# Order of the query tile blocks within a pair of attention heads: 6+1, 7+0, 4+3, 5+2 in place of 7+0, 6+1, 5+2, 4+3

## The chip, the cores and the metric

The kernel runs on one core of a Trainium2 chip. The metric is the device time of one execution in microseconds. The kernel before takes 1441.79 us (median of 3 runs, 1440.93 to 1442.77); lower is better.

## The reference

The input is x, four sequences of 1024 tokens with 256 channels, float32. It is normalised over the channels (xn), and the result is

```python
x = x + attention(xn) + einsum('bsi,oi->bso', xn, binarised(W_ffn)) + b_ffn
```

The attention has 16 heads with compressed keys, values and queries:

```python
kv_c = x @ W_kvd + b_kvd                       # 64 channels
keys = concat(heads(kv_c @ W_ku + b_ku), rope(heads(kv_c @ W_kr + b_kr)))    # 128 + 64 per head
q_c  = x @ W_qd + b_qd                         # 192 channels
q    = concat(heads(q_c @ W_qu + b_qu), rope(heads(q_c @ W_qr + b_qr)))
scores = einsum('bhqd,bhkd->bhqk', q, keys) / sqrt(192), masked above the diagonal
ctx = einsum('bhqk,bhkd->bhqd', softmax(scores), heads(kv_c @ W_vu + b_vu))
return ctx @ W_o + b_o
```

The mask is causal: query tile qt (128 rows) sees only key tiles 0 to qt.

## The kernel before

All matmuls keep float32 quality by splitting operands in a high and a low part (fp32r) and adding products. The 16 heads are handled in 8 pairs per sequence, so there are 4 x 8 = 32 pair steps. `LONG_SHORT` (line 48) cuts the 8 query tiles of a pair into 4 blocks, each of a long and a short tile: (7, 0), (6, 1), (5, 2), (4, 3). Each block has 9 key tiles per head in sum. Blocks are numbered g = 0 to 127; the position of a block in its pair is n = g % 4 (positions 0 to 3), and every table by n (which tiles, which output is stored) reads `LONG_SHORT[n]`.

What one block does:

- TensorE writes scores into two PSUM slots used in turn (`ring`), in four items: x = 0 is head 0 of the long tile, x = 1 head 0 of the short tile, x = 2 and 3 the same for head 1. An item is a mask matmul on its diagonal tile (L1457) and three matmuls (high x high, low x high, high x low) for each chunk of up to 512 key columns (L1474 to L1476). The mask of an item is issued within an earlier group of transposes and waits until the item two before it has left its slot.
- VectorE takes the scores out of PSUM and finds each row's minimum (L1035, function `minimum`; the signs are turned). ScalarE applies the exponent in place and sums the rows (L755, `exponent`).
- TensorE transposes the probabilities in five groups per block (L1499, `turn_group`). A group is up to two key tiles of both heads, four transposes; a long tile with 7 or 5 key tiles, or a short one with 1 or 3, ends with a single group of two transposes. The first group of a tile waits for the exponents of both heads. ScalarE copies the group out as the high part (L764), VectorE subtracts for the low part (L1045).
- TensorE weighs the compressed values with them (L1517, L1518, `weigh_group`) into u_ps; ScalarE and VectorE take that out in two parts (L769, L778, L1051); TensorE multiplies with the value and output weights (L1537, L1538, `output`); VectorE adds the result, scaled by one over the row sum, to `acc` (L1082).

The work is pipelined over blocks. Each engine has a function `sequence(g)` with one list per position n, written out by hand. While block g has its scores made, groups of block g - 1 are transposed and weighed and outputs of g - 2 are made. ScalarE's, VectorE's and TensorE's queues run in order. The lists of position 0 and 1 on TensorE also hold the projections for the next pair: keys for the rotary part (`k_rope`) at the start of position 0, q_x late in position 0, q_y early in position 1 (L1444). ScalarE takes them out (L670); SyncE swaps halves of them with four DMAs (L375); GpSimd does the rotary arithmetic (L347) and the low parts (L357); ScalarE makes high parts (L733, L737). In pairs 5 to 8 of a sequence the lists hold the next sequence's work: statistics and normalisation, its transposes (pair 6), down projections and ffn matmuls (pair 7), natural-order projections (pair 8).

Key columns per chunk: tile 4 has its two chunks 384 and 256 wide, the others 512 and the rest. For both blocks of positions 0 and 1 the long tile has four groups and the short one one; for positions 2 and 3 it is three and two, which the lists assume.

Of the kernel before, what the change touches and what calls it, by code (L numbers as in the profile page):

```python
# [38 lines left out]
NT = SEQ // P  # L39
# [5 lines left out]

LONG_SHORT = tuple((NT - 1 - n, n) for n in range(NT // 2))
BLOCKS = len(LONG_SHORT)
SCORE_ITEMS = 4  # L50
DRAIN = 3
# [3 lines left out]
KEY_COLUMN = {qt: P if qt == 4 else 0 for qt in range(NT)}  # L55
assert all((long + 2) // 2 + (short + 2) // 2 == GROUPS for long, short in LONG_SHORT)

# [74 lines left out]
def build(nc, x, W_kvd, b_kvd, W_ku, b_ku, W_vu, b_vu, W_kr, b_kr, W_qd, b_qd, W_qu, b_qu, W_qr, b_qr,  # L132
# [21 lines left out]
    with ExitStack() as ctx:  # L154
# [143 lines left out]
        def groups_of(g):  # L298

            return [(w, qt, kt, min(2, qt + 1 - kt)) for w, qt in enumerate(LONG_SHORT[g % BLOCKS])  # L300
                    for kt in range(0, qt + 1, 2)]

        def probs_of(g, w, h):

            long, short = LONG_SHORT[g % BLOCKS]
            return probs[g % 2][h][:, (long + 1) * P * w:][:, 0:((long, short)[w] + 1) * P]
# [54 lines left out]
        def _(sp):  # L361
# [65 lines left out]
            def store(b, n):  # L427

                sp.wait_ge(acc_ready, (((b + 1) * PAIRS - 1) * BLOCKS + n + 1) * 2)
                for qt in LONG_SHORT[n]:  # L430
                    sp.dma_start(out[b, qt * P:(qt + 1) * P, :], acc[:, qt, :]).then_inc(stored[n], 16)
# [551 lines left out]
        def _(dve):  # L983
# [40 lines left out]
            def minimum(g, x):  # L1024
# [4 lines left out]
                b, pair, n = g // (PAIRS * BLOCKS), g // BLOCKS % PAIRS, g % BLOCKS  # L1029
                qt, entry = LONG_SHORT[n][w], ("score", g, x)  # L1030
                keys, r = (qt + 1) * P, (g * SCORE_ITEMS + x) % 8
# [765 lines left out]
```

## Time and profile before

| | before |
|---|---|
| median of the runs | 1441.79 us |
| the profiled execution: its time / its span | 1437.33 / 1435.5 us |
| TensorE matmul busy | 1395.9 us (97%) |
| TensorE weight load busy | 1264.1 us (88%) |
| ScalarE busy | 1203.7 us (84%) |
| VectorE busy | 1152.2 us (80%) |
| GpSimd busy | 996.0 us (69%) |
| mean granted TensorE clock | 0.997 |

Rows of the profile name a line of the kernel, an engine, an operation and what it writes from what it reads. PE is TensorE's matmuls, PEld its weight loads, which run beside them; ACT is ScalarE, DVE VectorE, POOL GpSimd. Times in a timeline count from the span's start. A matmul's time there includes its way through the array, so the start-to-start distance of matmuls, not their own time, is what each costs in the stream.

### The profile page before, as it was taken

How to read it: one execution, taken by the hardware profiler on the slowest of the kernel's cores; microseconds unless marked ns; L12 is line 12 of the kernel's file. 1: busy time of each engine (PE TensorE's matmuls, PEld its weight loads, DVE VectorE, ACT ScalarE, POOL GpSimd, SP SyncE). 2: the span in 40 equal slices, each digit the busy share in tenths (PEclk: the TensorE clock that was granted, in tenths of full speed). 3: DMA queues.
4: the chain of work that ended last, by engine and by line, in shares of the span. 5: the costliest groups of instructions: out<-in, count | busy, mean ns of one | idle time of the engine just before them, and what ended most of it. 6: DMA issues, size and time to landing. Idle time of an engine off the chain costs nothing.

```text
span 1435.5 us, 27603 instructions
## 1 busy us (share of the span) xinstructions
PE 1395.9 (97%) x9786; PEld 1264.1 (88%) x9786; DVE 1152.2 (80%) x2708; ACT 1203.7 (84%) x2603; POOL 996.0 (69%) x573
## 2 busy tenths in 40 slices
PE   6989999999999999999999999999999999999997
PEld 4779999998898999988898999999889999999987
DVE  4858888876778888887687889887677888888887
ACT  4668888996888988898688888999778988888886
POOL 6886687777566767768765777777765777666750
PEclk9999999999999999999999999999999999999999
DMA  9752212212333222211333222221233322221100
GB/s 273 213 131 57 74 42 63 63 52 60 83 98 78 78 63 64 63 48 31 77 92 97 67 68 62 64 63 49 63 74 89 87 58 64 63 63 49 41 20 30
DMA packets 46958, 106.82 MB, mean 74 GB/s; under 512 B 9334, under 2 KB 17831, under 8 KB 46823
## 3 DMA queue, kind: packets, MB, share of 16 engines
q1 hardware_dynamic: 43360, 94.01, 25.7%
q0 software_dynamic: 3296, 11.01, 2.7%
q8 instruction: 80, 1.31, 0.4%
q14 instruction: 56, 0.45, 0.1%
q10 hardware_dynamic: 166, 0.03, 0.0%
HBM read 48.92 MB, written 9.96 MB: 41 GB/s over the span
## 4 chain that ended last, share of the span: by engine, by line
PE 77%; ACT 8%; POOL 6%; DVE 4%; DMA 3%; issue 1%; SPq 1%; POOLq 0%; DVEq 0%; ACTq 0%
PE turn L1499 15%; PE ring L1444 10%; PE u_ps L1517 8%; PE ring L1476 8%; PE ring L1475 8%; PE u_ps L1518 8%; PE ring L1474 8%; PE o_ps L1537 4%; PE o_ps L1538 4%; ACT probs L755 3%; PE ring L1457 2%; POOL k_rope L347 2%; PE ring L1389 1%; PE ring L1383 1%; ACT probs_hi L764 1%
## 5 line engine op out<-in xcount | busy, mean ns | idle before, releaser
L1035 DVE TENSOR_SCALAR_CACHE_REDUCE probs<-ring,c_t 128x1024 f32<-128x1024 f32 (+7 forms) x512 | 414.1, 810 | 99.6 <-PE ring L1476 95.4
L1045 DVE TENSOR_TENSOR probs_lo<-turn,probs_hi 128x512 fp32r<-128x512 f32 (+1 forms) x640 | 401.0, 630 | 69.3 <-ACT probs_hi L764 64.4
L764 ACT ACTIVATE probs_hi<-turn 128x512 fp32r<-128x512 f32 (+1 forms) x640 | 349.9, 550 | 110.0 <-PE turn L1499 103.4
L755 ACT ACTIVATE probs<-probs,row_min 128x1024 f32<-128x1024 f32 (+7 forms) x512 | 394.1, 771 | 11.8 <-DVE probs L1035 9.4
L1499 PE MATMUL turn<-ident,probs 128*128 128x128 f32 x2304 | 388.0, 275 | 6.3 <-ACT probs L755 4.0
L1517 PE MATMUL u_ps<-probs_hi,kv_nat 128*128 128x256 f32 x1152 | 313.5, 301 | 0.0
L1499 PEld LDWEIGHTS turn<-ident,probs 128*128 128x128 f32 x2304 | 282.9, 140 | 32.3 <-ACT probs L755 9.9
L1518 PE MATMUL u_ps<-probs_lo,kv_nat 128*128 128x256 f32 x1152 | 288.8, 280 | 0.0
L1474 PE MATMUL ring<-k_hi,q_hi 128*128 128x512 f32 (+3 forms) x768 | 275.8, 359 | 0.0
L1476 PE MATMUL ring<-k_hi,q_lo 128*128 128x512 f32 (+3 forms) x768 | 263.2, 343 | 0.0
L1475 PE MATMUL ring<-k_lo,q_hi 128*128 128x512 f32 (+3 forms) x768 | 262.6, 342 | 0.0
L1082 DVE SCALAR_TENSOR_TENSOR acc<-o_ps,row_inv,acc 128x256 f32<-128x256 f32 x480 | 230.1, 479 | 34.8 <-PE o_ps L1538 30.4
L1517 PEld LDWEIGHTS u_ps<-probs_hi,kv_nat 128*128 128x128 f32 x1152 | 219.1, 190 | 0.7 <-DVE kv_nat L1022 0.3
L1518 PEld LDWEIGHTS u_ps<-probs_lo,kv_nat 128*128 128x128 f32 x1152 | 218.4, 190 | 0.0
L357 POOL TENSOR_TENSOR k_lo<-k_rope,k_hi 64x1024 fp32r<-64x1024 f32 x62 | 148.2, 2390 | 50.1 <-ACT k_hi L733 47.7
L347 POOL TENSOR_TENSOR k_rope<-k_rope,cos 128x1024 f32<-128x1024 f32 x31 | 74.5, 2403 | 143.4 <-DMA swapped<-k_rope 143.1
L347 POOL TENSOR_TENSOR q_x<-q_x,cos 64x1024 f32<-64x1024 f32 x31 | 74.2, 2394 | 131.0 <-DMA swapped<-q_x 131.0
L1476 PEld LDWEIGHTS ring<-k_hi,q_lo 128*128 128x128 f32 x768 | 144.8, 189 | 13.9
L1474 PEld LDWEIGHTS ring<-k_hi,q_hi 128*128 128x128 f32 x768 | 146.6, 191 | 7.4
L347 POOL TENSOR_TENSOR swapped<-swapped,sin 128x1024 f32<-128x1024 f32 x62 | 148.7, 2398 | 4.9
L1475 PEld LDWEIGHTS ring<-k_lo,q_hi 128*128 128x128 f32 x768 | 145.4, 189 | 7.5
L1537 PE MATMUL o_ps<-wv,u_hi 128*128 128x256 f32 x512 | 143.6, 302 | 4.2 <-DVE acc L1082 2.3
(218 smaller groups left out, 2573.7 us busy)
## 6 DMA issues: line engine op xcount, KB each, us to landing
swapped<-k_rope SPq DMA_DIRECT2D x128, 128.0 KB, 2.3
wv<-wv_scratch SPq DMA_DIRECT2D x62, 256.0 KB, 4.1
wp<-wp_scratch SPq DMA_DIRECT2D x62, 192.0 KB, 3.5
wp<-wp_scratch SPq DMA_DIRECT2D x31, 256.0 KB, 3.2
swapped<-q_y SPq DMA_DIRECT2D x62, 128.0 KB, 2.3
swapped<-q_x SPq DMA_DIRECT2D x62, 128.0 KB, 2.4
k_hi<-qb_kv_hi SPq DMA_DIRECT2D x16, 256.0 KB, 3.7
k_lo<-qb_kv_lo SPq DMA_DIRECT2D x16, 256.0 KB, 4.8
```

Of the source, the lines that this page charges most:

```text
L347: engine.tensor_tensor(to, a, b, op).then_inc(rope_step, 1)
L755: act.activation(p, p, ACT.Exp, scale=-1.0, bias=row_min[:, r:r + 1], accum_out=row_sum[:, g % 4, w, h:h + 1]).then_inc(exp_ready, 1)
L764: act.activation(probs_hi[:, r % 4, 0:width], turn[r % 2][:, 0:width], ACT.Identity).then_inc(turned_hi, 1)
L1035: dve.tensor_scalar(probs_of(g, w, h), ring[slot_of(entry)][:, KEY_COLUMN[qt]:KEY_COLUMN[qt] + keys], c_t[b % 2][:, qt, ds(pair * 2 + h, 1 ...
L1045: dve.tensor_tensor(probs_lo[:, r % 4, 0:width], turn[r % 2][:, 0:width], probs_hi[:, r % 4, 0:width].bitcast(F32), ALU.subtract).then_inc ...
L1082: dve.scalar_tensor_tensor(out=acc[:, qt, :], in0=o_ps[:, h, :], scalar=inv, in1=start[:, qt, :], op0=ALU.mult, op1=ALU.add).then_inc((acc ...
L1474: pe.matmul(to, qh, kh[:, keys], start=not masked, stop=False, skip_group_check=masked)
L1475: pe.matmul(to, qh, kl[:, keys], start=False, stop=False, skip_group_check=masked)
L1476: mm = pe.matmul(to, ql, kh[:, keys], start=False, stop=True, skip_group_check=masked)
L1499: mm = pe.transpose(turn[r % 2][:, (2 * t + h) * P:(2 * t + h + 1) * P], probs_of(g, w, h)[:, kt * P:(kt + 1) * P], ident[:, :])
L1517: pe.matmul(u_ps[:, 0:2 * P], kv_nat[:, kt, :], probs_hi[:, r % 4, cols], start=(kt == 0), stop=False)
L1518: mm = pe.matmul(u_ps[:, 0:2 * P], kv_nat[:, kt, :], probs_lo[:, r % 4, cols], start=False, stop=(kt == qt))
```

## The change

One line changes: the order in which the pairs of tiles are listed. The same four blocks exist as before; the position of each within a pair of heads is another, and all lists by position now meet other tile sizes. The stores to DRAM by position follow.

```diff
-LONG_SHORT = tuple((NT - 1 - n, n) for n in range(NT // 2))
+LONG_SHORT = tuple((NT - 1 - n, n) for n in (1, 0, 3, 2))
```

Position 0 holds 6+1 (before: 7+0), position 1 holds 7+0 (6+1), position 2 holds 4+3 (5+2), position 3 holds 5+2 (4+3).

## Rows read from the trace of the kernel before

**Rows 1.** The page's first part: engine, busy us (share), number of instructions.
```profile
PE 1395.9 (97%) x9786; PEld 1264.1 (88%) x9786; DVE 1152.2 (80%) x2708; ACT 1203.7 (84%) x2603; POOL 996.0 (69%) x573
```

**Rows 2.** Waits, whole run: who waited for whom, us in total, times, longest.
```profile
POOL k_rope L347 <- DMA swapped<-k_rope: 143.1, 28, 8.7
...
PE ring L1457 <- ACT q_y L670: 4.0, 2, 3.1
PE turn L1499 <- ACT probs L755: 4.0, 7, 0.9
```

**Rows 3.** TensorE, groups by form: shapes and count, busy us, mean ns, idle before.
```profile
L1476 PE MATMUL ring<-k_hi,q_lo 128*128 128x512 f32 x320 | 126.5, 395 | 0.0
...
L1476 PE MATMUL ring<-k_hi,q_lo 128*128 128x384 f32 x192 | 65.1, 339 | 0.0
```

**Rows 4.** Timeline of TensorE, pair 18, position 2: start us, us, instructions.
```profile
830.35 0.27 PE L1499 MATMUL turn<-ident,probs 128*128 128x128 f32 x1
...
831.63 0.60 PE L1499 MATMUL turn<-ident,probs 128*128 128x128 f32 x4
831.98 0.37 PE L1517 MATMUL u_ps<-probs_hi,kv_nat 128*128 128x256 f32 x1
...
832.87 0.28 PE L1518 MATMUL u_ps<-probs_lo,kv_nat 128*128 128x256 f32 x1
...
833.10 0.28 PE L1518 MATMUL u_ps<-probs_lo,kv_nat 128*128 128x256 f32 x1
833.36 0.55 PE L1499 MATMUL turn<-ident,probs 128*128 128x128 f32 x3
```

**Rows 5.** ScalarE, groups by form: the exponent of 768 and of 640 elements.
```profile
L755 ACT ACTIVATE probs<-probs,row_min 128x768 f32<-128x768 f32 x64 | 59.3, 926 | 0.0
L755 ACT ACTIVATE probs<-probs,row_min 128x640 f32<-128x640 f32 x64 | 52.8, 825 | 0.2 <-DVE probs L1035 0.2
```

**Rows 6.** Timeline of ScalarE, pair 18, positions 2 and 3.
```profile
830.83 0.38 ACT L764 ACTIVATE probs_hi<-turn 128x256 fp32r<-128x256 f32 x1 [0.29 <-PE turn L1499]
...
832.29 0.92 ACT L755 ACTIVATE probs<-probs,row_min 128x768 f32<-128x768 f32 x1
833.12 0.18 ACT L755 ACTIVATION_READ_ACCUMULATOR probs<-probs,row_min 128x1 f32 x1
833.21 0.57 ACT L764 ACTIVATE probs_hi<-turn 128x512 fp32r<-128x512 f32 x1
...
842.33 0.19 ACT L755 ACTIVATION_READ_ACCUMULATOR probs<-probs,row_min 128x1 f32 x1
```

**Rows 7.** VectorE, groups by form: the minimum over 768 and 640 elements.
```profile
L1035 DVE TENSOR_SCALAR_CACHE_REDUCE probs<-ring,c_t 128x768 f32<-128x768 f32 x64 | 64.7, 1011 | 0.7 <-PE ring L1476 0.7
L1035 DVE TENSOR_SCALAR_CACHE_REDUCE probs<-ring,c_t 128x640 f32<-128x640 f32 x64 | 55.4, 865 | 2.2 <-PE ring L1476 2.2
```

**Rows 8.** Timeline of TensorE, pair 18 position 3, pair 19 position 0.
```profile
837.74 0.22 PE L1457 MATMUL ring<-mask_bf,ident_bf 128*128 128x128 bf16 x1
...
843.02 0.49 PE L1499 MATMUL turn<-ident,probs 128*128 128x128 f32 x3
```

**Rows 9.** Timeline of VectorE, pair 18, position 3.
```profile
837.06 0.08 DVE L1035 DVE_READ_ACCUMULATOR probs<-ring,c_t 128x1 f32 x1
```

**Rows 10.** Timeline, position 1 of pair 11 (first row) and of pair 19.
```profile
518.47 0.10 PEld L1457 LDWEIGHTS ring<-mask_bf,ident_bf 128*128 128x128 bf16 x1 [0.33 <-ACT q_y L670]
...
858.98 1.12 ACT L670 ACTIVATE q_y<-ring,bias_p 128x1024 f32<-128x1024 f32 x1 [0.55 <-PE ring L1444]
...
860.91 0.22 PE L1457 MATMUL ring<-mask_bf,ident_bf 128*128 128x128 bf16 x1
```

**Rows 11.** Timeline of TensorE, pair 16, position 3.
```profile
756.11 0.23 PE L1457 MATMUL ring<-mask_bf,ident_bf 128*128 128x128 bf16 x1 [0.94 <-DVE probs L1035]
```

**Rows 12.** Timeline of TensorE, pair 1, position 1.
```profile
94.89 0.29 PE L1457 MATMUL ring<-mask_bf,ident_bf 128*128 128x128 bf16 x1 [3.12 <-ACT q_y L670]
```

**Rows 13.** Busy us by engine (instructions), granted clock, DMA share, GB/s of a window.
```profile
94.00:99.00 5.00, 4.11 (x20) 3.81 (x20) 3.02 (x7) 3.97 (x9) 1.12 (x1) 0.66 0.56 115
```

## The prediction

> **What bounds the kernel now.** I read the page's busy times first, then who waited for whom, then the timelines of one ordinary pair in the middle of the run, pair 18 of 32, position by position. TensorE is busy 1395.9 of 1435.5 us [rows 1]. Its waits are few: the two kinds that this change touches, for the q_y eviction and for the exponent, sum to 4.0 us each [rows 2]. So TensorE's own issue stream is the bound, and only two things can move the time: the sum of that stream, and the small stalls in it. ScalarE matters although it is busy only 84% of the span. In the third and fourth block of a pair its instructions stand back to back, so what it finishes late there TensorE must wait for.
>
> **What is moved, and what it sums to.** The four blocks of a pair hold tiles 7+0, 6+1, 5+2, 4+3. The code that orders each engine's work belongs to the position (n = 0 to 3), not to the tiles. Now position 0 gets 6+1, 1 gets 7+0, 2 gets 4+3, 3 gets 5+2. Every instruction of a pair is still issued once, so the stream's sum stays. Inside a position these sizes change:
> - Scores: 128 key columns more or less on a tile change three matmuls by about 56 ns each [rows 3], 0.17 us; between 128 and 256 columns it is some 0.07 us.
> - The group of two score tiles that is not full. It holds one key tile: two transposes and two u_ps matmuls in place of four and four. It is the last group (index 4) of 7+0 and 5+2, index 3 of 6+1, index 2 of 4+3. A double group takes four transposes, 0.35 us from start to start (831.63 to 831.98 in rows 4), a single about 0.22 us less; a pair of u_ps matmuls is 0.23 us (832.87 to 833.10).
> - ScalarE: 128 more elements of exponent are 0.10 us [rows 5], a double group's eviction 0.57 against 0.38 us [rows 6]. VectorE: 128 more elements of the minimum are 0.14 us [rows 7].
>
> Summed on TensorE: position 0: +0.24, position 1: -0.24, position 2: +0.46, position 3: -0.46 us. As each stays attached to its place, the pair's sum is 0. I cost no DMA: SyncE issues the same transfers in the same order.
>
> **Position 2, the stall of every ordinary pair.** Now the first turn of the block's own probabilities (833.36, three transposes) waits for ScalarE's second long exponent, whose accumulator read ends at 833.12 + 0.18 = 833.30 [rows 4, 6]. TensorE was ready at 833.10 + 0.12 = 833.22, and the first transpose is followed by another 0.06 us of gap: 0.20 us per pair, in 23 of 32 pairs (not in pairs 6 to 8 of the first three batches). It is tempting to book this as gained, because the long tile there shrinks from 6 to 5 key tiles. But the chain starts elsewhere: from turn group 3 (830.35) through its eviction (830.83), the copy and the short tile's exponent, then the long one (832.29), all back to back. With the change group 3 is double (transposes +0.22, eviction +0.20), the short exponent is 512 in place of 384 (+0.10), the long one -0.10: chain +0.42. TensorE from the same point: group 3 +0.22, short scores +0.17, group 4 single -0.22, last weighing double +0.24: +0.41. Stall 0.2 us as before. Bounds: 0 (all of it gone) to 0.4.
>
> **Position 3 into position 0.** From that exponent on ScalarE runs without a gap to the end of position 3's second long exponent, 842.33 + 0.19 = 842.52; the turn that needs it starts at 843.02 [rows 6, 8]: 0.50 us of slack. With the change, after the position 2 stall: group 4's eviction -0.20, third exponent +0.10, position 3: long +0.10, group 2 -0.20, short -0.10, group 4 +0.20, long +0.10: sum 0.0. TensorE between the two points: position 3 is 0.46 shorter, the rest the same. So 0.46 of 0.50 us goes, and 0.04 is left, where a released transpose shows a lag of 0.06 (833.30 to 833.36). That is a stall of 0 to 0.15 us; I take 0.10, the lag and the 0.06 behind it that the like stall in position 2 shows, less 0.03 for a wait on the q_x eviction at the end of position 0 that goes. 0.07 x 23: +1.6 us. In the same block the mask matmul of the third score item sits at 837.74, 0.60 us after the minimum it needs (837.06 + 0.08) [rows 8, 9]. It comes 0.46 sooner (group 2 single -0.22, short scores -0.17, weighing of group 4 of the block two before -0.24, long scores +0.17), the minimum ends 0.05 later: 0.1 us is left, lag of 0.06 included, still no stall.
>
> **The q_y eviction in position 1.** ScalarE's backlog arrives at position 0 about 0.40 us later relative to TensorE (0.46, less 0.10 for the shorter last exponent, plus 0.05 for the minimum), so the k_rope eviction, its swap DMAs, the rope on GpSimd, k_hi, and then q_y all move by 0.40. On GpSimd this goes into its next wait for a swap, of which there are 28 with 143.1 us, 5.1 each [rows 2]. Position 1 starts 0.24 later. Usual q_y ends at 858.98 + 1.12 = 860.10, and the mask needs it at 860.91 [rows 10]: slack 0.81. With the change the mask comes 0.34 sooner in its position (single group 3 -0.22, short scores -0.07, weighing of group 4 of the block two before -0.23, long scores +0.17), and q_y 0.18 later, as its projection starts behind the longer scores: slack 0.28. That is enough in a usual pair. In 6 of the 31 pairs a swap DMA lands about 1.4 us late and the slack is gone already; one such stands at 518.47, where the load of the mask matmul sat idle for 0.33 us until q_y [rows 10]. There k_hi and q_y run back to back, 0.1 us later than now in the position, and the mask comes 0.35 sooner: 0.45 us longer each, +2.2 us for the five in ordinary places. The three pairs in which ScalarE also normalises the next batch there (pair 6 of a batch) have 0.35 of slack and lose 0.15 each: +0.5.
>
> **Once per batch and once per run.** Pair 8 of the first three batches: the mask in position 3 waits for the short minimum [rows 11]; the mask is reached 0.44 sooner, the minimum ends 0.06 sooner, and position 0 behind it then has no stall (-0.07): +0.3 each, +0.9 us. First pair: TensorE waits 3.12 us for q_y at 94.89 [rows 12], a chain from the residual on GpSimd that the order doesn't touch; 0.3 us of TensorE work passes from before this wait to behind it: +0.3. The drain of the last block runs with no scores to cover waits: its group 2 is double (transposes, eviction and subtraction, some 0.6 us by rows 4 and 6), its last group single (-0.6), its long exponent and minimum longer (+0.24), its short ones shorter: -0.5 to +1.2, I take +0.5, as the longer items come first and TensorE runs out of other work behind them.
>
> Sum: 1.6 + 2.2 + 0.5 + 0.9 + 0.3 + 0.5 = +6.0 us. The profiled execution took 1437.33 us (span 1435.5 and 1.8 around it), 4.5 below the median of the runs, 1441.79; 1437.3 + 6.0 = 1443.3 for a like execution. Carried to the median: 1441.8 + 6.0 = 1447.8.
>
> **A rule beside the trace.** In the first pair TensorE, idle for 3.12 us before 94.89, then ran at a mean granted clock of 0.66 between 94 and 99 us, one stretch at 1.2 GHz, the rest at 2.4; at most (1 - 0.66) x 5 = 1.7 us lost [rows 12, 13]. The Trainium skill, "TensorE: Matmul & The Clock Gate", Part 1, says that the throttled clock is the default and that activity releases it; the trace agrees. By that rule a wait that grows is a risk beyond its length: this one grows by 0.3 us, and a second low stretch would be worth up to 1.7 us by the rows. I leave it out of the sum.
>
> **Rivals.**
> - A: faster. The 0.20 us stall of position 2 vanishes and nothing takes its place: -0.2 x 23 = -4.6, and -0.03 x 31 = -0.9, against the +0.3 of the first pair: 1441.8 - 5.2 = 1436.6 us. It is decided by ScalarE's chain from turn group 3: it must end 0.15 us sooner against TensorE than I sum. For it: the long tile is smaller there. Against it: rows 6 have no gap in which the double eviction would fit.
> - B: no change. The small slacks hold (0.04 in position 0, 0.28 in position 1), the late swaps fall where there is room, and only the fixed terms stay, 0.9 + 0.3 + 0.5 = 1.7: 1443.5. For it: the sum of the stream is equal.
> - C: clearly slower. The thin slacks of position 3 and 0 both break: 0.15 us more at each in 23 pairs, 6.9 on top of the 6.0: 1454.7. VectorE would be the new bound in position 3: its first minimum has 768 elements there, it stands behind a subtraction, and both the mask and ScalarE's first exponent wait for it.
>
> **How the numbers follow.** Forecast case 0.50 (its own range 1445 to 1451), A 0.10, B 0.25, C 0.15. What this kernel's measurement tells from no change is 0.2%, 2.9 us. Slower: the forecast, C and a little of B, 0.64; same 0.26; faster 0.10. The range takes in B and part of C: 1441 to 1453.
>
> **What would show it.** In the changed trace of an ordinary pair: the first turn of position 2 still right behind an exponent; TensorE's wait for ScalarE in the first turn of position 0 near 0.1 us; the position 1 mask closer than 0.4 us to q_y's end, with waits for q_y grown from 4.0 us to 6 or more; positions lasting 13.8, 10.4, 9.0 and 6.7 us in place of 13.5, 10.6, 8.5 and 7.2. It is wrong if no exponent ends just before position 2's turn, or if the pair's period falls below 39.8 us.

## The result, and the profile after

The changed kernel takes 1451.15 us (median of 4 runs, 1450.46 to 1452.09), the kernel before 1442.28 us beside it (4 runs, 1440.93 to 1445.14): ratio 1.0069, 95% interval [1.0048, 1.0091]. It is slower, by 8.9 us between these medians, where +6.0 was forecast. (The ratio is given as recorded; the quotient of the two medians is 1.0062.) Run once more later, on the same chip as other experiments, it gave 1.0079 [1.0061, 1.0097]. The profiled execution took 1450.46 us (span 1448.7), 13.2 us of span more than the profiled execution of before.

The page's first part after, as [rows 1]:

```profile
PE 1404.0 (97%) x9786; PEld 1265.2 (87%) x9786; DVE 1148.8 (79%) x2708; ACT 1204.4 (83%) x2603; POOL 995.3 (69%) x573
```

The instruction counts are those of before. TensorE's busy time nevertheless grew by 8.1 us. A row's own time (0.27 us for a transpose) is longer than its distance to the next one (0.11 us), so a wait shorter than the difference leaves no idle time in the profile, and matmuls at the lower clock take longer and count as busy too. Busy time is no measure of work here.

The waits of the whole run after (who waited for whom, us in total, times, longest), as [rows 2]:

```profile
POOL k_rope L347 <- DMA swapped<-k_rope: 150.5, 28, 10.1
...
PE ring L1457 <- ACT q_y L670: 8.1, 5, 4.7
PE ring L1457 <- DVE probs L1035: 6.6, 7, 1.4
PE turn L1499 <- ACT probs L755: 4.8, 8, 1.0
```

The wait for q_y doubled (4.0 to 8.1 us), and the forecast wanted 6 or more. That is weaker than it looks: 4.7 of the 8.1 us are the first pair's (3.1 before), and in a second execution of the same kernel, below, this line reads 1.7 us. The wait for VectorE's minimum (5.7 us before) is the line that the forecast did not put first.

**An ordinary pair.** Lengths of the positions, from the first matmul of a position's list on TensorE to that of the next, median over pairs 1 to 4 of batches 2 to 4 (the last row is the sum of the four):

| position | before | forecast | after |
|---|---|---|---|
| 0 | 13.53 | 13.8 | 13.85 |
| 1 | 10.59 | 10.4 | 10.34 |
| 2 | 8.53 | 9.0 | 9.08 |
| 3 | 7.17 | 6.7 | 6.74 |
| pair | 39.82 | | 40.01 |

Pair 18 after, position 2: ScalarE's second long exponent, and the turn and masks on TensorE behind it (as [rows 4, 6]):

```profile
839.99 0.82 ACT L755 ACTIVATE probs<-probs,row_min 128x640 f32<-128x640 f32 x1
840.71 0.18 ACT L755 ACTIVATION_READ_ACCUMULATOR probs<-probs,row_min 128x1 f32 x1
...
840.95 0.55 PE L1499 MATMUL turn<-ident,probs 128*128 128x128 f32 x3
```

The read ends at 840.89 and the turn starts 0.06 later: the stall of position 2 is still there. Position 3 of the same pair, VectorE, ScalarE and TensorE (as [rows 8, 9]):

```profile
843.24 0.68 DVE L1045 TENSOR_TENSOR probs_lo<-turn,probs_hi 128x512 fp32r<-128x512 f32 x1
843.84 1.01 DVE L1035 TENSOR_SCALAR_CACHE_REDUCE probs<-ring,c_t 128x768 f32<-128x768 f32 x1
844.77 0.09 DVE L1035 DVE_READ_ACCUMULATOR probs<-ring,c_t 128x1 f32 x1
...
844.32 0.59 ACT L764 ACTIVATE probs_hi<-turn 128x512 fp32r<-128x512 f32 x1
844.89 0.94 ACT L755 ACTIVATE probs<-probs,row_min 128x768 f32<-128x768 f32 x1
...
844.78 0.27 PE L1499 MATMUL turn<-ident,probs 128*128 128x128 f32 x1
844.91 0.23 PE L1457 MATMUL ring<-mask_bf,ident_bf 128*128 128x128 bf16 x1
```

The minimum ends at 844.86. The mask follows at 844.91 and the exponent at 844.89: where before [rows 8, 9] the mask came 0.60 us after its minimum, it now comes 0.05 after it. The exponent ends the row at the start of position 0 of pair 19, where the first turn had 0.50 us of slack in [rows 6, 8]:

```profile
850.00 0.19 ACT L755 ACTIVATION_READ_ACCUMULATOR probs<-probs,row_min 128x1 f32 x1
...
850.25 0.98 PE L1499 MATMUL turn<-ident,probs 128*128 128x128 f32 x7
```

It has none: 850.19 to 850.25. And q_y in position 1 of pair 19, as [rows 10]:

```profile
866.64 1.12 ACT L670 ACTIVATE q_y<-ring,bias_p 128x1024 f32<-128x1024 f32 x1 [0.59 <-PE ring L1444]
...
868.06 0.22 PE L1457 MATMUL ring<-mask_bf,ident_bf 128*128 128x128 bf16 x1
```

868.06 less 867.76 is 0.30 us of slack; 0.28 was forecast (0.81 before).

**Where a swap lands late**, pair 14, position 1, first ScalarE, then the load and the mask on TensorE:

```profile
639.48 2.14 ACT L733 ACTIVATE k_hi<-k_rope 64x1024 fp32r<-64x1024 f32 x2 [1.41 <-POOL k_rope L347]
642.65 1.09 ACT L670 ACTIVATE q_y<-ring,bias_p 128x1024 f32<-128x1024 f32 x1
...
643.79 0.10 PEld L1457 LDWEIGHTS ring<-mask_bf,ident_bf 128*128 128x128 bf16 x1 [1.70 <-ACT q_y L670]
643.80 0.23 PE L1457 MATMUL ring<-mask_bf,ident_bf 128*128 128x128 bf16 x1 [1.51 <-ACT q_y L670]
```

**Pair 8 of a batch, position 3**, TensorE, as [rows 11] (the second row is the same place one batch later):

```profile
759.75 0.27 PE L1499 MATMUL turn<-ident,probs 128*128 128x128 f32 x1
761.36 0.23 PE L1457 MATMUL ring<-mask_bf,ident_bf 128*128 128x128 bf16 x1 [1.34 <-DVE probs L1035]
...
1106.22 0.23 PE L1457 MATMUL ring<-mask_bf,ident_bf 128*128 128x128 bf16 x1 [1.36 <-DVE probs L1035]
```

The windows behind them (busy us by engine and instructions, then the granted clock, DMA share, GB/s):

```profile
760.00:765.00 5.00, 3.66 (x27) 3.46 (x27) 2.44 (x8) 3.27 (x8) 4.79 (x3) 0.89 0.03 8
1105.00:1110.00 5.00, 3.78 (x26) 3.60 (x27) 2.32 (x9) 3.13 (x7) 4.79 (x3) 0.86 0.02 3
```

The clock fell from 2.4 to 1.2 GHz at 763.9 and at 1108.6 us, each time for 3.4 us. Before, it fell nowhere between the first pair and the end. Position 3 lasts 11.56 and 11.58 us with the fall and 10.00 in the first batch, where none came: 1.5 us each.

**The 13.2 us of span by part**, pair by pair against the profiled execution of before, with the forecast's terms:

| part | forecast | profiled execution |
|---|---|---|
| ordinary pairs (21), their own period | +1.6 | 0.2 each, +4.2 |
| swaps landing late in them, and one stall of before in pair 9 (0.7) that is not there | +2.2 | +0.3 |
| pair 6 of a batch (3) | +0.5 | +0.6 |
| pair 7 of a batch (3) | 0 | +1.7 |
| pair 8 of a batch (3) | +0.9 | +1.4, and +3.0 by the clock |
| first pair | +0.3 | +1.0 |
| last pair and drain | +0.5 | +0.9 |

The parts sum to 13.1; rounding and 0.03 us ahead of the first pair make up the rest.

### The profile page after: what moved, and what is told of

Same layout as the page of the kernel before. It is cut to its first block, busy times and chain, and to the rows that moved or that the text cites. A ratio compares the mean times of both kernels' runs of the same rounds, so it can differ in the third digit from the quotient of the medians.

```text
span 1448.7 us, 27603 instructions
## 1 busy us (share of the span) xinstructions
PE 1404.0 (97%) x9786; PEld 1265.2 (87%) x9786; DVE 1148.8 (79%) x2708; ACT 1204.4 (83%) x2603; POOL 995.3 (69%) x573
## 3 DMA queue, kind: packets, MB, share of 16 engines
q8 instruction: 80, 1.31, 0.4%
## 4 chain that ended last, share of the span: by engine, by line
PE 73%; ACT 10%; POOL 6%; DVE 4%; DMA 4%; issue 1%; SPq 1%; POOLq 0%; DVEq 0%; ACTq 0%
PE turn L1499 15%; PE ring L1444 9%; PE u_ps L1517 7%; PE ring L1476 7%; PE ring L1475 7%; PE u_ps L1518 7%; PE ring L1474 7%; PE o_ps L1537 3%; PE o_ps L1538 3%; ACT probs L755 3%; POOL k_rope L347 2%; PE ring L1457 2%; DMA swapped<-k_rope 2%; ACT probs_hi L764 2%; PE ring L1389 1%; PE ring L1383 1%
## 5 line engine op out<-in xcount | busy, mean ns | idle before, releaser
L1035 DVE TENSOR_SCALAR_CACHE_REDUCE probs<-ring,c_t 128x896 f32<-128x896 f32 (+7 forms) x512 | 413.5, 809 | 115.5 <-PE ring L1476 112.9
L755 ACT ACTIVATE probs<-probs,row_min 128x896 f32<-128x896 f32 (+7 forms) x512 | 394.7, 772 | 12.8 <-DVE probs L1035 9.1
```

What stands on the lines that cost most here:

```text
L755: act.activation(p, p, ACT.Exp, scale=-1.0, bias=row_min[:, r:r + 1], accum_out=row_sum[:, g % 4, w, h:h + 1]).then_inc(exp_ready, 1)
L1035: dve.tensor_scalar(probs_of(g, w, h), ring[slot_of(entry)][:, KEY_COLUMN[qt]:KEY_COLUMN[qt] + keys], c_t[b % 2][:, qt, ds(pair * 2 + h, 1 ...
```

## The experiments

All were timed against the kernel before on the same chip. The experiments ran in three groups; the median of the kernel before was 1438.55, 1438.48 and 1439.01 us in them (single executions 1434.99 to 1444.86).

**The two halves of the change, each alone.** Positions 0 and 1 exchanged:

```diff
-LONG_SHORT = tuple((NT - 1 - n, n) for n in range(NT // 2))
+LONG_SHORT = tuple((NT - 1 - n, n) for n in (1, 0, 2, 3))
```

> Only positions 0 and 1 are exchanged (6+1, 7+0, 5+2, 4+3). Theory 1 (sizes at fixed places decide, through ScalarE's back-to-back chain): position 2 now transposes the groups of 7+0, so turn group 3 is double there (+0.42 us on ScalarE's chain) while TensorE gains only 0.23 us before the turn that waits for the exponent: the stall of position 2 grows from 0.20 to about 0.4 us in ordinary pairs, position lengths about 13.3, 10.6, 8.95, 6.95 us, the pair 40.0 us; q_y's slack about 0.5 us, so late swaps cost 0.2 us more each. Sum +5 to +7 us on the kernel before (+0.4%). Theory 2 (each exchange costs about half of what the full change costs): +4.5 us, with waits spread over positions 0 and 3 too. Theory 3 (the cost of the full change is mostly the clock falling behind the wait in position 3 of pair 8): the wait there is 1.3 us or less here; if the clock falls, 1.5 us each time, otherwise next to nothing over theory 1.

1450.9 us, 1.0085 [1.0071, 1.0100]. Positions 13.42, 10.61, 9.20 and 6.94 us, the pair 40.17. The whole loss of the change is in this half, and its ordinary pair is longer than with both halves. Theory 1 has the mechanism: the stall of position 2 (the wait at the turn and the gap behind it) grew from 0.20 to 0.38 us. It was too low in the sum, +12 us against +5 to +7; one fall of the clock (1.5 us) and 0.6 us in each pair 7 are part of the difference.

Positions 2 and 3 exchanged, `for n in (0, 1, 3, 2)`:

> Only positions 2 and 3 are exchanged (7+0, 6+1, 4+3, 5+2). Theory 1: in position 2 group 3 stays single, ScalarE's two exponents before the waiting turn sum to the same, and TensorE has 0.17 us more scores in front of it: the stall falls from 0.20 to under 0.05 us; position 0's first turn keeps about 0.2 us of slack, the q_y slack is about 0.6 us. Ordinary pair 39.65 us, sum -3 to -5 us on the kernel before (-0.3%), unless the wait in position 3 of pair 8 (1.3 us expected) lets the clock fall, 1.5 us each. Theory 2 (half the cost each): +4.5 us. Theory 3 (clock): no fall, then within 0.1% of before or faster.

1437.13 us, 0.9988 [0.9976, 1.0000]: at most a small gain, 1.4 us between the medians where -3 to -5 were expected. Positions 13.99, 10.34, 8.38 and 6.93 us, the pair 39.64. The stall of position 2 is down to 0.04 us, as theory 1 wanted. Per ordinary pair +0.35 and -0.18 make +0.17, of the +0.2 of both together: the halves add, nearly.

**The mask in position 3 of pair 8.** The natural-order projection, whose slot is free earlier, stands behind that wait. In the changed kernel it is issued first:

```diff
-                    turn_group(g - 1, 2, (g, 2))
                     if pair == 7:
                         begin("natural", b + 1, 1)
+                    turn_group(g - 1, 2, (g, 2))
```

> The changed kernel (6+1, 7+0, 4+3, 5+2) with one step moved on TensorE: in position 3 of pair 8 the natural-order projections (1.8 us of matmuls) are issued before the group of transposes whose mask waits for the short minimum, not behind it. The wait of 1.5 us there should be covered whole, three times, and with it the falls to 1.2 GHz behind it (1.5 us each, two in the profiled execution). Theory 3 and my account: -4.5 us for the waits and -3 us for the clock, together -7 to -8 us on the changed kernel, so within 0.2% of before. If the clock falls for another reason than this wait, only -4.5 us and the falls stay in the trace.

1442.48 us, 1.0027 [1.0014, 1.0040]. The position lasts 8.66 to 8.68 us in all three batches (10.00, 11.56, 11.58), and the clock falls nowhere in mid-run. By the ratios (1.0069 and 1.0079 down to 1.0027) 6 to 7.5 us were to be had at one place that comes three times.

The same edit in the kernel before:

> The kernel before with the same step moved. There the wait is 1.1 us three times and the clock does not fall: -3.3 us (-0.23%) if TensorE's stream is the bound behind it, with no change in the number of falls. If the wait only moves on to the next turn of position 0, nothing is gained.

1435.74 us, 0.9982 [0.9969, 0.9995]. The position is 1.11 shorter three times, and position 0 behind it 0.36 longer. So some 2.6 of the 6 to 7.5 us (0.7 to 4.5 by the interval) were there to be had before the change already; the other 3.5 to 5 us are what the changed order lost here: 0.4 us more wait three times, and the clock.

**What makes the clock fall.** The changed kernel, with 14 transposes of the identity (result unused) ahead of that mask (the call passes `fill=14` in pair 8 of the first three batches and nothing elsewhere):

```diff
                         if (t, h) == (tiles - 1, 1):
+                            for _ in range(fill):
+                                pe.transpose(turn[r % 2][:, 2 * P:3 * P], ident[:, :], ident[:, :])
```

> The changed kernel with 14 transposes of the identity, whose result nobody reads, issued ahead of the waiting mask matmul in position 3 of pair 8 (three times in the run). They take some 1.2 us and stand in a wait of 1.5 us. Theory (behind this wait TensorE's granted clock falls to 1.2 GHz for 3.4 us in some executions, 1.5 us each, because TensorE stood still; the wait is set by VectorE's minimum and not by TensorE): position 3 of pair 8 lasts 10.0 us in all three batches, no clock fall there, the run 0 to 4.5 us below the changed kernel, 3 likeliest; ratio to the kernel before about 1.005. Rival (the fall has another cause, such as the amount of work before it): falls stay in one or two of three, position 3 at 11.5 there, ratio as the changed kernel or 0.1% above.

TensorE in position 3 of pair 16, and the window over it:

```profile
762.14 0.27 PE L1502 MATMUL turn<-ident,probs 128*128 128x128 f32 x1
762.25 1.69 PE L1499 MATMUL turn<-ident 128*128 128x128 f32 x14
763.77 0.22 PE L1458 MATMUL ring<-mask_bf,ident_bf 128*128 128x128 bf16 x1
```
```profile
760.00:766.00 6.00, 6.00 (x53) 5.83 (x52) 4.76 (x14) 4.63 (x9) 4.25 (x3) 1.00 0.13 44
```

From the transpose ahead to the mask it is 1.63 us, where it was 1.61 without the fill: the wait is as long, but TensorE works. The position lasts 9.99, 9.99 and 10.00 us, and the clock stays at 2.4 GHz three times of three. The time does not show it: 1449.64 us, 1.0075 [1.0055, 1.0095], as the changed kernel. In the profiled execution the first pair took 3.4 us more than in the changed kernel's, and a late swap cost 1.6. So the fill's worth is seen in the position's length only. That it held the clock up is likely, not shown: the unfilled wait of this length, counted below, had no fall in 7 of 15 places either, so that three of three would come by chance about once in ten times. The Trainium skill, "TensorE: Matmul & The Clock Gate", Part 4, says that transposes do not count as TensorE being busy in the way that matmuls do. This trace speaks against it, by three places. A row of the kernel before speaks against it more plainly:

```profile
19.81 3.54 PE L1372 MATMUL ring<-ident,xn 128*128 128x128 f32 x16
```

These 16 transposes are all that TensorE began from 19.81 to 23.18 us, and the clock rose to 2.4 GHz at 23.13. In the stretch they stand 0.21 us from start to start, where transposes of an ordinary pair stand 0.11 us apart.

The kernel before, in the old order, with its wait made as long as the changed kernel's:

```diff
+                    if pair == 7 and b + 1 < NB:
+                        dve.tensor_reduce(waste[:, b:b + 1], cos[:, 0:384], AX.X, ALU.add)
                     minimum(g, 1)
```

> The kernel before, in its old order, with one more reduction on VectorE (384 elements, result unused) ahead of the short minimum of head 0 in position 3 of pair 8, in three batches. It lengthens TensorE's wait at the mask there from 1.1 us by some 0.45 us to about what the changed kernel has (1.5). Theory (the length of the wait brings the clock fall, whatever the order): TensorE's granted clock falls behind it in two or three of the three places, position 3 there lasts 10.04 + 0.45 without and 12.1 with a fall; the run is 4 to 6 us above the kernel before, ratio 1.003 to 1.004. Rival (the fall comes from the amount of work around, the smaller position 3 of the changed order): no fall, 1.4 us, ratio 1.001.

1443.2 us, 1.0029 [1.0016, 1.0043]. Position 3 is 0.46, 2.02 and 0.46 us longer. The window behind the second:

```profile
762.00:768.00 6.00, 6.00 (x40) 5.97 (x39) 3.03 (x8) 3.66 (x8) 4.37 (x2) 0.72 0.00 0
```

One fall in three, not two or three; but the old order has it too, once the wait is longer, and the time lies above the rival's 1.001. The count over all profiled executions at this place, by the length of the wait (the distance from start to start less the usual 0.11 us): none of 3 at 1.10 us (before), none of 3 at 1.29 (positions 2 and 3 exchanged), 1 of 3 at 1.31 (positions 0 and 1 exchanged), 8 of 15 at 1.50 to 1.55 us (the changed kernel twice, 2 and 1; the short copy below, 1; the keys last, 3; this one, 1), none of 3 filled.

The timed runs say the same without a timeline, as each has its mean granted clock on record. The time lost by it, (1 - clock) x span, is 8.5 us in the mean for the kernel before in this group (17 runs), 11.4 with the longer wait (12), 10.6 for the changed kernel (6) and 10.9 with the short copy (6). The difference of 3.0 us for the longer wait (95% interval 0.5 to 5.5) is what its time has above the 1.4 us of added waiting. With the natural-order projection first it is 7.3 (changed) and 7.5 us (before), against 7.6 in their group. Filled it is 7.7 against 7.0, and with the keys last 10.9 against 7.0.

But the length of the wait alone doesn't decide it. In the run with the keys last (further below), position 1 of pairs 9, 17 and 25 has a wait of 2.3 us by the same measure, longer than any here, and the clock stayed up all three times:

```profile
815.67 0.39 PE L1517 MATMUL u_ps<-probs_hi,kv_nat 128*128 128x256 f32 x1 [2.01 <-DVE kv_nat L1022]
```

Five waits of 1.4 to 1.7 us for q_y in pairs 14 and 17 of five executions brought no fall either. Over all places it is 11 falls behind 29 waits of 1.3 us or more, and none in mid-run behind a shorter one. What else decides stays open.

**The changed kernel once more:**

> The changed kernel once more, unaltered, for a comparison on the same chip with the others of this call and for another look at its clock. Theory: ratio 1.006 to 1.009; falls of the clock in mid-run behind the 1.5 us waits of pair 8, in one to three of three places; late swaps in other pairs than in the first look, three to six of them in ordinary places. Rival (the falls of the first look were chance): none here.

1450.63 us, 1.0079 [1.0061, 1.0097]. One fall in mid-run, at 1107.1 us. Its waits for q_y in other than the first pair are 0.29, 0.19, 1.09, 0.16 and 0.30 us, 2.0 in sum, where the first profiled execution had 4.5 and the kernel before 1.8. They stand in pairs 5, 6, 14, 22 and 29, the same as in the first but for pair 2; the lengths differ.

**The chain on ScalarE from position 2 to position 0.** In the changed kernel one copy on ScalarE is cut from 256 to 64 columns:

```diff
-                    u_again(g - 1, 0)
+                    u_again(g - 1, 0, 64)
                     high_queries(g, 0)
```

> The changed kernel; in position 2 ScalarE's second copy of u (u_again of the long tile, L778) copies 64 of 256 columns, so the products of that tile lack part of their low halves. It takes about 0.2 us out of the back-to-back chain on ScalarE between the exponent that position 2's turn waits for and the one that position 0's first turn waits for. Theory (an ordinary pair is 0.2 us longer because this chain has no slack left: 0.11 us at position 0's first turn, some at the mask in position 3): position 0 is 0.1 to 0.15 us shorter, the pair 39.87 in place of 40.0, in all 3 to 4 us, ratio to the kernel before 1.004 to 1.005. Rival (VectorE's minimum sets the exponent's start, and the chain only looks tight): the pair stays at 40.0 and the ratio at 1.007.

1451.37 us, 1.0083 [1.0064, 1.0102], the pair still 40.0: no gain. The theory is refuted. The same place as above, here VectorE and ScalarE:

```profile
846.44 1.01 DVE L1035 TENSOR_SCALAR_CACHE_REDUCE probs<-ring,c_t 128x768 f32<-128x768 f32 x1
847.38 0.08 DVE L1035 DVE_READ_ACCUMULATOR probs<-ring,c_t 128x1 f32 x1
...
846.77 0.59 ACT L764 ACTIVATE probs_hi<-turn 128x512 fp32r<-128x512 f32 x1
847.49 0.94 ACT L755 ACTIVATE probs<-probs,row_min 128x768 f32<-128x768 f32 x1
```

The copy took 0.16 us less (0.42 to 0.26), and ScalarE's eviction is over at 847.36. The exponent still starts at 847.49, 0.03 behind the minimum's end (847.46). What was saved became a gap of 0.13 us. In this run VectorE's first minimum of position 3, 768 elements behind a subtraction, holds the chain that ends at position 0's first turn. In the changed kernel both chains end within 0.05 us of each other, and so its trace alone looks as if ScalarE did it. No run shortens the minimum, so it isn't shown that VectorE's part alone would give anything.

**The late swaps.** The changed kernel, with q_y taken out ahead of the keys' high parts:

```diff
-                    high_keys(g)
                     if pair == 5:
                         next_apply(b + 1, 2)
                     evacuate(g, QUERY_Y)
+                    high_keys(g)
```

> The changed kernel, with ScalarE taking q_y out ahead of the two high parts of k_rope at the end of its position 0 list, instead of behind them. Theory (a late swap transfer of k_rope costs TensorE time only because q_y's eviction stands behind k_hi on ScalarE, and the changed order took 0.45 us of the slack there): the four or five waits for q_y in ordinary places (0.7 to 1.7 us each, 4.1 in all in the profiled execution) and the 0.16 us in the three pairs 7 go: 3 to 5 us below the changed kernel, ratio to the kernel before 1.0035 to 1.005. Rival (the swaps' lateness comes through q_y's own swap or the keys, later in the pair): same as the changed kernel, 1.0065 to 1.009. Second rival: q_y's eviction now makes ScalarE stand idle for the projection and delays its whole queue: worse than 1.009.

1497.81 us, 1.0415 [1.0393, 1.0438]: 47 us slower than the changed kernel. The theory misses by far, and the second rival has it. ScalarE there:

```profile
853.14 1.12 ACT L670 ACTIVATE q_y<-ring,bias_p 128x1024 f32<-128x1024 f32 x1 [2.64 <-PE ring L1444]
854.15 2.13 ACT L733 ACTIVATE k_hi<-k_rope 64x1024 fp32r<-64x1024 f32 x2
```

The two high parts, 2.13 us, had filled the time in which ScalarE waits for q_y's projection (0.59 us of idle were left, above). Moved behind it they stand in front of the turn groups' evictions: the idle time grows to 2.64, and position 1 from 10.34 to 12.18 us in each ordinary pair. The edit does not tell how much the late swaps cost.

**Towards a better kernel.** Positions 2 and 3 exchanged, with the natural-order projection issued first (as above) and the ffn matmuls of pair 7 (position 2) too:

```diff
-                    turn_group(g - 1, 2, (g, 2))
                     if pair == 6:
                         begin("linear", b + 1, 0)
+                    turn_group(g - 1, 2, (g, 2))
```

> Only positions 2 and 3 exchanged (7+0, 6+1, 4+3, 5+2), and two once-per-batch steps issued before the turn group they stood behind: the natural-order projection in position 3 of pair 8, and the ffn matmuls in position 2 of pair 7. Theory (the changed order loses by its first two positions and by the batch steps, and the other two positions gain): 0.17 us less in each of some 23 pairs (3.9), pair 8 position 3 about 1.1 to 1.4 us less in three batches (3.9), pair 7 position 2, where TensorE stands some 2.0 us, about 0.7 less in three batches (2.1): 9 to 10 us below the kernel before, ratio 0.993 to 0.994, and no clock fall in mid-run. Rival (the waits are only handed on to the next block): ratio 0.997 to 0.999, what the exchange or the one step alone gave (0.9988, 0.9982).

1433.68 us, 0.9969 [0.9955, 0.9983]: 4.8 us below, half of what was expected. Pair 8 is 1.15 us shorter three times, but pair 7 is 0.5 longer. TensorE in position 2 of pair 7:

```profile
362.15 0.23 PE L1457 MATMUL ring<-mask_bf,ident_bf 128*128 128x128 bf16 x1 [1.07 <-DVE x_sb L997]
```

The wait of 0.6 us at one mask went, and one of 1.07 came at the next, which waits until VectorE has taken out the ffn product that now stands two items ahead. With the keys last as well:

> As the kernel with only positions 2 and 3 exchanged and the two once-per-batch steps hoisted, plus q_y's eviction ahead of the high parts of k_rope on ScalarE. In this order q_y has 0.8 us of slack in an ordinary pair, so only late swaps matter: in the profiled execution of the kernel before its waits for q_y come to 2.05 us in ordinary places beside the first pair's. Theory: 1 to 2 us below the same kernel without this step, ratio to before 0.992 to 0.993. Rival (ScalarE waits for the projection and loses): 1 to 3 us above it.

1485.51 us, 1.0322 [1.0301, 1.0344], for the same reason as above. Here the clock falls twice at another place, in position 1 of pairs 17 and 25, behind an idle time of 1.89 us (a wait of 2.1 us by the measure above); behind the same wait in pair 9 it doesn't.

Without the step that lost, positions 2 and 3 exchanged and the natural-order projection first:

> Only positions 2 and 3 exchanged, and only the natural-order projection of pair 8 hoisted (the kernel with both steps hoisted lost 0.55 us in each pair 7 by the other step, three times). Theory: its terms add: 0.15 us less in 19 ordinary pairs (2.9), 0.1 in each pair 7 (0.3), 1.15 in each pair 8 (3.5), against 0.13 more in pairs 5 and 6 of three batches (0.8) and 0.36 in the last pair: 5.5 us below the kernel before, ratio 0.996, and 1 to 1.5 us below the kernel with both steps hoisted (0.9969). Rival (the loss in pair 7 goes elsewhere once the step is back): 0.997 to 0.998.

1431.42 us, 0.9949 [0.9931, 0.9967]: faster than the kernel before and the changed one, 7.6 us below the former where the terms sum to 5.5, which the interval holds. That it also beats the kernel with both steps first (0.9969) is not shown, as the intervals overlap. The ordinary pair is 39.64 us, pair 7 55.2 and pair 8 43.1 (44.3 before).

## Why the prediction was right, point by point

- *The stream's sum stays, and each position gains or loses by its tiles.* Right: all four lengths are within 0.1 us.
- *Position 2 keeps its stall.* Right, 0.23 us for 0.20, still behind the exponent. It is ScalarE's chain from turn group 3 that keeps it. The two halves show it: with the group double and TensorE's work not grown as much the stall is 0.38 us (positions 0 and 1 exchanged), with the group single it is 0.04 us (positions 2 and 3 exchanged), and there the position is 0.15 us shorter than before.
- *Position 3 into position 0.* Right in place, and mis-sized: +0.07 per pair was booked, 0.11 us is lost at the first turn with the gap behind it. Its cause was half of the truth. The text followed ScalarE alone ("sum 0.0"). The short copy showed that relieving ScalarE gains nothing, because VectorE's minimum, some 0.14 us longer there, ends as late; it had been named only as what would decide rival C. The smaller losses beside it (0.05 at the first turn of position 2, where the slack is 0.07 us, 0.03 at the mask of position 3, a few hundredths in position 2) are read from the trace; no run separates them. The term measured 0.2 x 21 = 4.2 us in place of 1.6.
- *q_y in position 1.* The slack was forecast to 0.02 us. The price, 2.2 us for five late swaps, can't be confirmed: the waits for q_y outside the first pair were 4.5 us in one execution of the changed kernel and 2.0 in the next, against 1.8 before. How late a swap lands, and in part which one, changes from one execution to the next (pair 14 waits in each of them, 1.70 and 1.09 us). The term is an expectation over executions, and one trace of before was taken for a constant.
- *Pair 8, +0.9.* The wait was right: 1.10 to 1.50 us, 0.4 each. What stood behind it was not in the sum. The clock fell behind it in 2 of 3 places, then in 1 of 3, at 1.5 us each. The text weighed such a fall, but only for the first pair, where the changed kernel has the same two falls as before (3.4 us each, from 67.6 and 94.9 us, against 67.5 and 94.8). The wait to look at was the one that grew in mid-run. The two kernels with the projection first show the whole place to be worth 3.5 to 5 of the 9 to 11.6 us.
- *Pair 7* was not in the sum and cost 0.55 three times. Position 0 waits for its turn there as in an ordinary pair and a little more; I have the lengths (+0.5, -0.2, +0.5, -0.2 by position) but no experiment on the cause.
- *First pair, last pair and drain*: +1.9 in place of +0.8; the last pair has no projections beside it, and its position 0 is 0.72 us longer in place of 0.33.
- *The rivals.* A (faster) needed position 2's stall to go; it did not. B's 1443.5 lies below the lowest run. C's mechanism, VectorE's minimum in position 3, is at work, but what is lost there is 0.1 us and not 0.15 at two places; 1454.7 is above the highest run.

Between the medians 8.9 and 11.6 us were measured, between the two profiled executions 13.2: the kernel before's was one of its faster ones (1437.33 us against 1438.5 to 1442.3 in the median). Against the 13.2 the forecast's +6.0 lacked 2.6 us for the ordinary pairs, 3.0 for the clock and 0.5 for the rest of pair 8, 1.7 for pair 7 and 1.1 for both ends, and held 1.9 too much for late swaps. With the late swaps at what this execution shows the forecast would have been +4.1, so that its nearness to the measured change is in part luck.

## What to carry to other kernels

A price by slack has to be worked out for every engine that feeds the waiting instruction: cut a little work out of the one you suspect, and if a gap opens behind it and nothing starts sooner, another engine holds it as well. Where TensorE is the bound, sort its waits by length and look first at those over a microsecond, even if they come three times in a run; hoist work that doesn't depend on them, and ask of each hoisted item who must take it out before the next may start. Work that fills an engine's idle time looks free to move, and is not: what it filled must be filled again.

## What the runs showed of the hardware that was not expected

- TensorE's clock can fall to 1.2 GHz for 3.4 us behind a single wait of 1.3 to 2.1 us in an otherwise full stream: in 9 of 18 such places in position 3 of pair 8, in 2 of 11 elsewhere, and not behind three waits of 2.3 us. A fall costs 1.5 us, about the wait's own length.
- Transposes count for the clock: 16 of them with nothing between preceded its rise at 23.13 us.
- Much of the spread of this kernel's runs is the clock: over the timed runs of the kernel before, time and mean granted clock go together with a correlation of -0.92, -0.89 and -0.84 in the three groups (29, 17 and 17 runs), in the first group from 1444.86 us at 0.990 to 1435.7 to 1437.5 us at 0.997. The profiled executions place it in the first 100 us. The code there is the same in the kernel before and in the one with a longer wait in pair 8. In the first, the granted clock is 0.94 between 45 and 100 us, and the second pair starts at 116.4 us; in the second it is 0.84, and the second pair starts at 122.1. The rows of the two:

```profile
45.00:100.00 55.00, 46.94 (x261) 38.58 (x260) 37.76 (x66) 32.50 (x102) 45.23 (x70) 0.94 0.62 163
```
```profile
45.00:100.00 55.00, 45.89 (x233) 37.21 (x232) 39.10 (x57) 27.51 (x93) 42.29 (x71) 0.84 0.59 152
```

A comparison of two profiled executions must leave this stretch out, or it puts up to 5.7 us down to the change.
